# Attention value products taken by pairs of key tiles, denominator sums with them, closing sum one head step sooner

## Chip, cores and metric

One core of one Trainium2 chip runs the whole program. The metric is the device time of one execution in microseconds (us), the median of several. Engine names are those of the profile: PE is TensorE (its matmuls; PEld its weight loads), DVE is VectorE, ACT is ScalarE, POOL is GpSimd, SP is SyncE, which here only issues DMAs.

## What is computed

A decoder layer with three residual blocks, each followed by a layer norm. The change touches only the first, a self attention of 16 heads over 2 batches of 2048 rows with 512 features:

```python
dots = jnp.einsum('bhid,bhjd->bhij', q, k) * scale
dots = jnp.where(causal_mask, -jnp.inf, dots)
attn = jax.nn.softmax(dots, axis=-1)
out = jnp.einsum('bhij,bhjd->bhid', attn, v)
```

Behind it come a cross attention on 77 context rows and a mixture of eight expert networks. The profile has the projections first (to 312 us), then the attention (312 to 1347 us), then the second half.

## The kernel before

`self_attention` goes through 8 groups: 2 batches times 4 groups of 4 heads (a head has 32 features). A group has 4 chunks `c` of 512 query rows, and chunk `c` has 4(c+1) key tiles `kt` of 128 keys; its last four lie on the diagonal, where only 512, 384, 256 and 128 of the queries are needed. That makes 40 tiles (`KU`) and, with a head each, 160 head steps (`VU`) in a group. I write (3,5) for chunk 3, key tile 5. Two groups make a lap, a loop body of 320 steps; a lap starts at step `TAIL` (52).

All engines walk through the same numbered steps `s`, each with its own instructions in a fixed order, and wait for one another by semaphores. A lag says how many steps behind its first matmul a piece of work is issued. `tile_at(s, lag, ...)` gives the tile k whose fourth head step was `lag` steps ago, so it answers at s = 4k+3+lag, and `chunk_at` does so for the last tile of a chunk.

- PE, `scores` (L865, on the diagonal also L868): at step p the transposed scores of one tile and head go to one of three banks of `st_ps` (`RING`), once ACT has read the item three before.
- PE, `aux` (L851): the same products the other way round, for the row maxima of chunks to come, about one in a step, into three banks of `s_ps`. DVE reads each (L804 a full 512 columns, L808 with the mask); PE waits for the item three before. The first `aux` item of a step goes out before the value products, the others behind them. At the end of a chunk's maxima there is a "rows" item (L843), which ACT and DVE turn into two rows of `q_pair`.
- ACT (L762): the exponential of each score bank into `probs`, which holds five tiles (`NP`).
- PE, `values` (L885), lag `VALUES` = 4: the four heads of a tile side by side, 32 columns of the array each, in float32 (two matmul instructions a head), added up in `o_ps`.
- The softmax denominators. Most tiles are in `POOLED`: POOL adds their `probs` (L637) into `total`, one tile at a time, lag 1. Seven tiles of a group are not ((1,2), (2,2), (2,5), (3,2), (3,5), (3,8), (3,11)); for them PE makes `sums` (L899) with a block of ones, lag `SUMS` = 6, again four heads side by side. `totals` (L909), lag `TOTALS` = 12, closes a chunk with one such product over `total`, and waits for POOL's last add of that chunk.
- Behind it, each at its lag counted from `TOTALS`: ACT copies the sums out (`TAKEN[1]`), three small DMAs and a DVE reciprocal spread their inverse, POOL scales the output (`SCALED`, L647), ACT rounds it to half precision (`UPPER`, L777, eight steps later), POOL subtracts (`LOWER`, L652, three more steps), SP stores it. In POOL's step the add comes first, then `SCALED`, then `LOWER`; in ACT's step the exponential comes first, `UPPER` last.

With `TOTALS` = 12, `SCALED` comes at 4k+41, `UPPER` at 4k+49 and `LOWER` at 4k+52 for a chunk that ends with tile k.

Of the kernel before, what the change touches and what calls it, by code (L numbers as in the profile page):

```python
# [401 lines left out]
def self_attention(nc, S, x_rows, q_parts, k_parts, v_rows, o_parts, inv_rows):  # L402
# [29 lines left out]
    NP = 5  # L432
    RING = 3

    VALUES, SUMS = 4, 6
    TOTALS = 12
    TAKEN = VALUES + 1, TOTALS + 1
    DEN_MOVED = TAKEN[1] + 1
    INVERTED = DEN_MOVED + 8
# [78 lines left out]
    def unit_at(s, lag, first, end):  # L518

        p = s - lag  # L520
        return None if (first is not None and p < first) or (end is not None and p >= end) else p

    def tile_at(s, lag, first, end):

        p = unit_at(s, lag, first, end)
        return p // HG if p is not None and p % HG == HG - 1 else None

    def chunk_at(s, lag, first, end):

        k = tile_at(s, lag, first, end)  # L530
        return k // NKU * CPB + CHUNK_OF[k % NKU] if k is not None and k % NKU in CHUNK_OF else None
# [3 lines left out]
    def aux_at(s, first, end):  # L535

        if first is not None:
            reached = [AHEAD + (done_by(TAIL) - AHEAD) * n // TAIL for n in (s, s + 1)]
        else:
            reached = done_by(s), done_by(s + 1)  # L540
        return [n for n in range(*reached) if end is None or n < 2 * NAUX]

    with ExitStack() as stack:
# [286 lines left out]
        def _(pe):  # L830
# [3 lines left out]
            def aux(i, n):  # L834
                what, c, unit = AUX[n % NAUX]
                k = n // NAUX * CPB + c
                slot, a = n % (2 * NAUX) % RING, k // CPB % 2

                pe.wait_ge(s_read.sem, s_read.at(i, before(n, RING, 2 * NAUX)))
                if what == "rows":  # L840

                    pe.wait_ge(max_ready.sem, max_ready.at(i, k))
                    nc.tensor.transpose(s_ps[0:HG * TT, slot, 0:P], row_max[:].rearrange("p h j -> p (h j)"),  # L843
                                        ident_f[:]).then_inc(s_ready.sem, 1)
                    return
                j, h, s = unit
                if j == h == s == 0:

                    pe.wait_ge(qk_loaded[a][c], 6 * 16 * (i + k // (2 * CPB) + 1))
                width = CH if s < c else (j + 1) * P  # L850
                nc.tensor.matmul(s_ps[:, slot, 0:width], q_pair[a][0:NR, c, h, j * P:(j + 1) * P],  # L851
                                 k_pair[a][0:NR, h, s * CH:s * CH + width], start=True,
                                 stop=True).then_inc(s_ready.sem, 1)

            def scores(i, p):
                c, kt, h = VU[p % NVU]
                a, slot = p // NVU % 2, p % (2 * NVU) % RING
                if kt == h == 0:

                    k = p // NVU * CPB + c  # L860
                    pe.wait_ge(rows_moved[k % 2], stored_at(2 * (CPB * i + k // 2 + 1)))
                off = max(kt - c * TT, 0) * P
                pe.wait_ge(exp_done.sem, exp_done.at(i, before(p, RING, 2 * NVU)))
                diagonal = kt >= c * TT
                last = nc.tensor.matmul(st_ps[:, slot, off:], k_pair[a][:, h, kt * P:(kt + 1) * P],  # L865
                                        q_pair[a][:, c, h, off:], start=True, stop=not diagonal)
                if diagonal:
                    last = nc.tensor.matmul(st_ps[:, slot, off:off + P], ident[:], future[:], start=False, stop=True)  # L868
                last.then_inc(st_ready.sem, 1)
# [3 lines left out]
            def values(i, k):  # L873


                c, kt = KU[k % NKU]
                a, off = k // NKU % 2, max(kt - c * TT, 0) * P
                final = k % NKU == LAST_TILE[c]
                if kt == 0:
                    if c == 0:  # L880
                        pe.wait_ge(v_loaded[a], 16 * (i + k // (2 * NKU) + 1))
                    pe.wait_ge(o_taken.sem, o_taken.at(i, k // NKU * CPB + c - 1))
                pe.wait_ge(exp_done.sem, exp_done.at(i, HG * k + HG - 1))
                for h, out in enumerate(heads):
                    last = nc.tensor.matmul(o_ps[out, off:], v_sb[a][:, kt, out], probs[:, k % NP, h, off:],  # L885
                                            start=(kt == 0), stop=final)
                if k % NKU in POOLED[c]:
                    last.then_inc(pv_done.sem, 1)

            def sums(i, k):  # L890

                c, kt = KU[k % NKU]
                if k % NKU in POOLED[c]:
                    return
                opens = all(n in POOLED[c] for n, (x, _) in enumerate(KU) if x == c and n < k % NKU)
                if opens:
                    pe.wait_ge(den_taken.sem, den_taken.at(i, k // NKU * CPB + c - 1))
                for h, out in enumerate(heads):
                    last = nc.tensor.matmul(den_ps[out, :], ones[:], probs[:, k % NP, h], start=opens, stop=False)  # L899
                last.then_inc(pv_done.sem, 1)  # L900

            def totals(i, c):

                opens = all(n in POOLED[c % CPB] for n, (x, _) in enumerate(KU) if x == c % CPB)
                if opens:
                    pe.wait_ge(den_taken.sem, den_taken.at(i, c - 1))
                pe.wait_ge(added.sem, added.at(i, adds_upto(c // CPB * NKU + LAST_TILE[c % CPB]) - 1))
                for h, out in enumerate(heads):
                    last = nc.tensor.matmul(den_ps[out, :], ones[:], total[:, c % 2, h], start=opens, stop=True)  # L909
                last.then_inc(den_ready.sem, 1)  # L910

            def step(i, s, first, end):
                p = unit_at(s, 0, first, end)
                if p is not None:
                    scores(i, p)
                todo = aux_at(s, first, end)
                for n in todo[:1]:
                    aux(i, n)
                k = tile_at(s, VALUES, first, end)
                if k is not None:  # L920
                    values(i, k)
                k = tile_at(s, SUMS, first, end)
                if k is not None:
                    sums(i, k)
                c = chunk_at(s, TOTALS, first, end)
                if c is not None:
                    totals(i, c)
                for n in todo[1:]:
                    aux(i, n)

            pe.wait_ge(const_ready, 2)
            for n in range(AHEAD):
                aux(0, n)
            pe.wait_ge(factors_ready, 2)
            laps(pe, step)


# [581 lines left out]
def layer(nc, x_rows, xT, ctxT, mask, wqkvT, woutT, bout, wq, bq, wk, bk, wv, bv, wo, bo, w1, b1, w2, b2, centroids,  # L1519
          routeT, out):  # L1520

    dram = lambda name, shape, dt: nc.dram_tensor(name, shape, dt).ap()
    q_parts, k_parts, o_parts = (dram(n, [2, D, N], F16) for n in ("q_parts", "k_parts", "o_parts"))
    v_rows = dram("v_rows", [N, D], F32)
    inv_rows = dram("inv_rows", [2, HG, CH], F32)
    w_parts = dram("w_parts", [2 * KT, P, 2, KT * D], F16)
    k_blocks, v_ctx = dram("k_blocks", [B, P, NG * HG * S2], F32), dram("v_ctx", [B, S2, D], F32)
    with ExitStack() as stack:
        S = lasting(nc, stack)
        smalls = [(S["bout_bc"][:], bout.partition_broadcast(P)), (S["bo_bc"][:], bo.partition_broadcast(P)),  # L1530
                  (S["bq_sb"][:], bq), (S["b1_sb"][:], b1), (S["b2_sb"][:], b2)]
        project(nc, S, xT, wqkvT, ctxT, wk, wv, woutT, wq, wo, w1, w2, centroids, routeT, smalls, bk, bv,
                q_parts, k_parts, v_rows, w_parts, k_blocks, v_ctx)
        self_attention(nc, S, x_rows, q_parts, k_parts, v_rows, o_parts, inv_rows)
        second_half(nc, S, x_rows, o_parts, mask, w_parts, k_blocks, v_ctx, out)
# [68 lines left out]
```

## Time and profile before

| | before |
|---|---|
| time, median of 3 (lowest, highest) | 2633.9 us (2633.06, 2635.76) |
| the profiled execution: its time, its span | 2630.97 us, 2629.2 us |
| PE busy over the span | 2430.0 us (92%) |
| DVE busy | 1715.9 us (65%) |
| ACT busy | 1097.3 us (42%) |
| POOL busy | 1119.8 us (43%) |
| matmuls | 13556 |
| granted TensorE clock, mean | 0.958 |

Busy shares are averages over three different stages; the attention is read by itself below. A matmul's duration holds its way through the array (a 512 column one shows 0.38 us, while the next one starts 0.22 us after it), so a PE that is "busy" all the time can still be waiting a little before each matmul. In a timeline the number in square brackets is the idle time of that engine before the instruction, with what ended it; "x2" after an instruction means two of them merged into a line, whose time then spans both.

### The profile page before, as it was taken

What the parts mean: (1) busy time and instruction counts of PE and PEld (TensorE: products, weight loads), DVE (VectorE), ACT (ScalarE), POOL (GpSimd) and SP (SyncE); (2) the same over time, 40 slices, a digit from 0 to 9 for tenths busy, and PEclk for the clock granted to TensorE, in tenths of its full rate; (3) what the DMA queues carried; (4) which work ended last, traced back from release to release, by engine and by line L of the source; (5) the groups of instructions that cost most, each with busy time, mean ns of one, the idle gap of its engine ahead of it and who ended that gap; (6) DMA issues with size and microseconds to landing.
All of it is one profiled execution on the core that took longest, in us unless ns stands there. A gap on an engine that the chain in (4) does not pass through costs nothing. (4 is left out here: it accounts for less than half of the span.)

```text
span 2629.2 us, 42902 instructions
## 1 busy us (share of the span) xinstructions
PE 2430.0 (92%) x13556; PEld 1018.3 (39%) x13556; DVE 1715.9 (65%) x3957; ACT 1097.3 (42%) x2066; POOL 1119.8 (43%) x404
## 2 busy tenths in 40 slices
PE   8999799999999999999956799999999999999998
PEld 3444223332333233323213354444445454454543
DVE  4443687776777677767405477767677776767665
ACT  4331256665666566666623242332324232322420
POOL 0000379988898989898952111102111111101100
PEclk9999799999999999999977899999999999999999
DMA  7864312212121212140021101010100101010000
GB/s 250 294 212 156 89 38 54 58 42 59 42 58 42 63 38 76 28 111 20 25 93 60 45 1 62 1 46 18 41 22 1 63 1 46 17 45 17 1 17 17
DMA packets 130506, 155.66 MB, mean 59 GB/s; under 512 B 19838, under 2 KB 98174, under 8 KB 129245
## 3 DMA queue, kind: packets, MB, share of 16 engines
q1 hardware_dynamic: 130269, 152.69, 18.9%
q8 instruction: 126, 2.06, 0.3%
q14 instruction: 111, 0.91, 0.1%
HBM read 99.96 MB, written 52.17 MB: 58 GB/s over the span
## 5 line engine op out<-in xcount | busy, mean ns | idle before, releaser
L762 ACT ACTIVATE probs<-st_ps 128x512 f32<-128x512 f32 (+3 forms) x1280 | 605.3, 536 | 359.0 <-PE st_ps L865 206.6
L637 POOL TENSOR_TENSOR total<-total,probs 128x2048 f32<-128x2048 f32 (+3 forms) x200 | 706.3, 3531 | 77.8 <-ACT probs L762 65.6
L804 DVE TENSOR_REDUCE seg_max<-s_ps 128x1 f32<-128x512 f32 x768 | 506.2, 684 | 143.4 <-PE s_ps L851 139.9
L865 PE MATMUL st_ps<-q_pair,k_pair 98*128 98x512 f16 (+3 forms) x1280 | 445.5, 362 | 36.6 <-ACT probs L762 22.7
L851 PE MATMUL s_ps<-k_pair,q_pair 96*128 96x512 f16 (+3 forms) x1280 | 446.0, 363 | 31.9 <-DMA q_pair<-q_parts 11.2
L1429 PE MATMUL fps<-x2T,w_p_hi 128*128 128x512 f16 x1024 | 317.3, 379 | 0.0
L885 PE MATMUL o_ps<-probs,v_sb 128*32 128x512 f32 (+3 forms) x2560 | 309.0, 556 | 0.0
L808 DVE CUSTOM_DVE_ANT_0 s_ps<-s_ps,later 128x384 f32<-128x384 f32 (+3 forms) x512 | 250.4, 497 | 89.1 <-issue 85.9
L1429 PE MATMUL fps<-w_p_hi,hT 128*128 128x512 f16 x1024 | 306.1, 381 | 0.0
L865 PEld LDWEIGHTS st_ps<-q_pair,k_pair 98*128 98x128 f16 x1280 | 124.8, 99 | 357.7 <-ACT probs L762 264.7
L1133 POOL TENSOR_TENSOR rstd<-rstd,keep_power 128x4 f32<-128x4 f32 x24 | 26.1, 1090 | 552.0 <-DVE rstd L1254 552.0
L1148 POOL TENSOR_TENSOR soft<-soft,ssum 128x1232 f32<-128x1232 f32 x32 | 72.9, 2287 | 384.4 <-DVE ssum L1284 384.4
L851 PEld LDWEIGHTS s_ps<-k_pair,q_pair 96*128 96x128 f16 x1280 | 126.9, 100 | 227.3 <-DVE seg_max L804 111.4
L1216 ACT ACTIVATE hidden<-fps,keep_b_sb 128x512 f32<-128x512 f32 x128 | 86.4, 686 | 303.7 <-PE fps L1429 303.4
L1391 DVE SCALAR_TENSOR_TENSOR x<-fps,gates_un,x 128x512 f32<-128x512 f32 x256 | 183.9, 745 | 36.2 <-PE fps L1429 33.8
L1429 PE MATMUL fps<-w_p_lo,hT 128*128 128x512 f16 x512 | 194.6, 380 | 0.0
L1429 PE MATMUL fps<-x2T,w_p_lo 128*128 128x512 f16 x512 | 194.0, 379 | 0.0
L637 POOL TENSOR_TENSOR total<-probs 128x2048 f32<-128x2048 f32 (+1 forms) x32 | 136.4, 4263 | 52.8 <-ACT probs L762 52.8
L1380 DVE TENSOR_SCALAR hT<-hidden 128x512 f16<-128x512 f32 x128 | 86.0, 672 | 107.6 <-ACT hidden L1216 107.0
L1429 PEld LDWEIGHTS fps<-x2T,w_p_hi 128*128 128x128 f16 x1024 | 100.2, 98 | 128.8 <-DVE x L1391 5.9
L1429 PEld LDWEIGHTS fps<-w_p_hi,hT 128*128 128x128 f16 x1024 | 98.1, 98 | 131.0 <-issue 20.8
L1187 ACT ACTIVATE soft<-soft 128x1232 f32<-128x1232 f32 x32 | 39.4, 1231 | 200.4 <-DVE soft L1277 200.4
(164 smaller groups left out, 3403.8 us busy)
## 6 DMA issues: line engine op xcount, KB each, us to landing
k_pair<-k_parts SPq DMA_DIRECT2D x96, 128.0 KB, 3.6
q_pair<-q_parts SPq DMA_DIRECT2D x96, 128.0 KB, 4.7
x_raw<-xT_in SPq DMA_DIRECT2D x8, 1024.0 KB, 6.3
q_parts<-qk_out SPq DMA_DIRECT2D x32, 256.0 KB, 3.6
k_parts<-qk_out SPq DMA_DIRECT2D x32, 256.0 KB, 3.9
piece_raw<-w_in SPq DMA_DIRECT2D x8, 1024.0 KB, 8.7
v_rows<-v_out SPq DMA_DIRECT2D x32, 256.0 KB, 2.2
w_parts<-piece_cut SPq DMA_DIRECT2D x8, 1024.0 KB, 5.6
```

Of the source, the lines that this page charges most:

```text
L637: last = nc.gpsimd.tensor_tensor(summed[:, :, off:], other[:, :, off:], probs[:, k % NP, :, off:], ALU.add)
L762: nc.scalar.activation(probs[:, k % NP, h, off:], st_ps[:, p % (2 * NVU) % RING, off:], ACT.Exp, scale=SCALE).then_inc(exp_done.sem, 1)
L804: nc.vector.reduce_max(highest, s_ps[:, slot], AX.X).then_inc(s_read.sem, 1)
L808: nc.vector.tensor_tensor_reduce(s_ps[:, slot, 0:width], s_ps[:, slot, 0:width], later[:, CH - width:CH], 1.0, MASKED, ALU.add, ALU.max, h ...
L851: nc.tensor.matmul(s_ps[:, slot, 0:width], q_pair[a][0:NR, c, h, j * P:(j + 1) * P], k_pair[a][0:NR, h, s * CH:s * CH + width], start=True ...
L865: last = nc.tensor.matmul(st_ps[:, slot, off:], k_pair[a][:, h, kt * P:(kt + 1) * P], q_pair[a][:, c, h, off:], start=True, stop=not diagonal)
L885: last = nc.tensor.matmul(o_ps[out, off:], v_sb[a][:, kt, out], probs[:, k % NP, h, off:], start=(kt == 0), stop=final)
L1148: nc.gpsimd.tensor_tensor(soft[:, j], soft[:, j], ssum[:, j, :].rearrange("p (h a) -> p h a", a=1).broadcast_to([P, H, S2]), ALU.mult).the ...
L1216: nc.scalar.activation(hidden[:, n % 2], fps[:, (u * NUNIT + f) % FB], ACT.Gelu, bias=W["b1_sb"][:, n:n + 1], scale=UN).then_inc(gelu_done ...
L1380: nc.vector.tensor_scalar(hT[:, 0, e % 2, j], hidden[:, n % 2], XS, None, ALU.mult).then_inc(h_hi.sem, 1)
L1391: nc.vector.scalar_tensor_tensor(x2[q][:, j], bank, gates_un[q][:, j, e:e + 1], x2[q][:, j], ALU.mult, ALU.add).then_inc(added.sem, 1)
L1429: last = nc.tensor.matmul(bank, lhs(a, t), rhs(b, t), start=(n == 0), stop=(n == len(steps) - 1))
```

## The change

```diff
-    VALUES, SUMS = 4, 6
-    TOTALS = 12
+    VALUES = 4
+    TOTALS = 11
     TAKEN = VALUES + 1, TOTALS + 1
     DEN_MOVED = TAKEN[1] + 1
...
                 for n in todo[:1]:
                     aux(i, n)
                 k = tile_at(s, VALUES, first, end)
-                if k is not None:
-                    values(i, k)
-                k = tile_at(s, SUMS, first, end)
-                if k is not None:
-                    sums(i, k)
+                if k is not None and k % 2:
+                    for n in (k - 1, k):
+                        values(i, n)
+                        sums(i, n)
                 c = chunk_at(s, TOTALS, first, end)
                 if c is not None:
                     totals(i, c)
```

The value products of an even tile wait for those of the odd tile behind it and go out in the same step, 4k+7 with k odd; a plain sum of either tile stands right behind its value products. The closing sum moves from step 4k+15, where it stood directly behind the value products of tile k+2, to step 4k+14, by itself. Every lag that is counted from `TOTALS` shrinks by one step: `SCALED` 4k+40, `UPPER` 4k+48, `LOWER` 4k+51, and `TAIL`, where a lap starts, 51. No arithmetic is added or taken away.

## Rows read from the trace of the kernel before

**Rows 1.** The attention stretch: busy time (count) by engine, granted clock, DMA share, GB/s

```profile
core 0: us, PE busy (x) PEld busy (x) DVE busy (x) ACT busy (x) POOL busy (x), PEclk, DMA share, GB/s
311.70:1346.70 1035.00, 970.33 (x6309) 312.23 (x6301) 724.08 (x2301) 642.11 (x1397) 918.17 (x302) 0.96 0.19 48
```

**Rows 2.** Timeline around one value product, PE and DVE: start us, us, instruction

```profile
410.78 0.28 PE L851 MATMUL s_ps<-k_pair,q_pair 96*128 96x256 f16 x1
411.00 1.07 PE L885 MATMUL o_ps<-probs,v_sb 128*32 128x512 f32 x8
411.99 0.39 PE L865 MATMUL st_ps<-q_pair,k_pair 98*128 98x512 f16 x1
412.64 0.69 DVE L804 TENSOR_REDUCE seg_max<-s_ps 128x1 f32<-128x512 f32 x1 [0.68 <-PE s_ps L851]
```

**Rows 3.** Timeline of PE: value product and closing sum in one step

```profile
534.36 1.06 PE L885 MATMUL o_ps<-probs,v_sb 128*32 128x512 f32 x8
535.25 1.04 PE L909 MATMUL den_ps<-total,ones 128*32 128x512 f32 x8
536.22 0.39 PE L865 MATMUL st_ps<-q_pair,k_pair 98*128 98x512 f16 x1
```

**Rows 4.** Views by tile: counts, durations min/median/max ns, forms

```profile
L885 PE MATMUL o_ps<-probs,v_sb x2560: 272/592/1063, 311.4 to 1334.0; 128*32 128x512 f32 x137, 128*32 128x384 f32 x20, 128*32 128x128 f32 x20, 128*32 128x256 f32 x20
L899 PE MATMUL den_ps<-probs,ones x448: 592/605/617, 340.1 to 1328.1; 128*32 128x512 f32 x150
L909 PE MATMUL den_ps<-total,ones x256: 592/592/1061, 333.1 to 1346.7; 128*32 128x512 f32 x128
```

**Rows 5.** Timeline of PE: first score products of (3,5) and of (3,9)

```profile
543.71 0.38 PE L865 MATMUL st_ps<-q_pair,k_pair 98*128 98x512 f16 x1
...
556.49 0.39 PE L865 MATMUL st_ps<-q_pair,k_pair 98*128 98x512 f16 x1
```

**Rows 6.** Timeline of DVE: two full reductions; a masked one of 384 columns

```profile
339.85 1.28 DVE L804 TENSOR_REDUCE seg_max<-s_ps 128x1 f32<-128x512 f32 x2
...
417.31 0.56 DVE L808 CUSTOM_DVE_ANT_0 s_ps<-s_ps,later 128x384 f32<-128x384 f32 x1
417.79 0.14 DVE L808 DVE_READ_ACCUMULATOR2_ANT seg_max<- 128x1 f32 x1
```

**Rows 7.** Timeline of POOL in the third group, from (2,3) to (3,3)

```profile
628.91 4.54 POOL L637 TENSOR_TENSOR total<-total,probs 128x2048 f32<-128x2048 f32 x1 [4.71 <-ACT probs L762]
633.40 1.16 POOL L652 TENSOR_TENSOR o_out<-o_sb,o_out 128x512 f16<-128x512 f32 x1
634.51 18.39 POOL L637 TENSOR_TENSOR total<-total,probs 128x2048 f32<-128x2048 f32 x4
652.86 1.27 POOL L647 TENSOR_TENSOR o_sb<-o_raw,inv 128x512 f32<-128x512 f32 x1
654.08 7.21 POOL L637 TENSOR_TENSOR total<-total,probs 128x1536 f32<-128x1536 f32 x3
...
662.37 4.54 POOL L637 TENSOR_TENSOR total<-probs 128x2048 f32<-128x2048 f32 x1
670.09 4.54 POOL L637 TENSOR_TENSOR total<-total,probs 128x2048 f32<-128x2048 f32 x1 [3.19 <-ACT probs L762]
```

**Rows 8.** Timeline of ACT and of PE in the same group, at (3,0)

```profile
654.16 0.63 ACT L777 ACTIVATE o_out<-o_sb 128x512 f16<-128x512 f32 x1 [2.95 <-POOL o_sb L647]
...
655.01 0.39 PE L865 MATMUL st_ps<-q_pair,k_pair 98*128 98x512 f16 x1 [2.17 <-ACT probs L762]
```

**Rows 9.** A stretch behind (3,0) with its granted clock, columns as in rows 1

```profile
655.78:662.61 6.83, 6.83 (x29) 1.73 (x26) 5.40 (x24) 4.05 (x8) 6.67 (x5) 0.50 0.10 23
```

**Rows 10.** Timelines of the second group: POOL, then PE

```profile
489.93 1.17 POOL L652 TENSOR_TENSOR o_out<-o_sb,o_out 128x512 f16<-128x512 f32 x1
...
491.27 1.04 PE L909 MATMUL den_ps<-total,ones 128*32 128x512 f32 x8
...
523.16 0.61 PE L865 MATMUL st_ps<-q_pair,k_pair 98*128 98x512 f16 x1 [2.96 <-ACT probs L762]
```

## The prediction

> **What bounds the kernel now.** I first read the table of windows, to see which engines fill the attention [rows 1]: in 1035 us PE counts 970 us busy, POOL 918, DVE 724, ACT 642. So two engines may set the pace, and the change touches both: PE's order directly, POOL's through the lags. The second half and the projections aren't touched.
>
> Then the timeline of PE around one value product [rows 2]. A score product of 256 columns starts at 410.78 and needs 0.11 us, yet the value product behind it starts at 411.00, not at 410.89: 0.11 us lost on the way in (0.09 to 0.11 elsewhere). Eight instructions then take until 411.99, 0.99 us. What one such product needs by itself is told by the place where two stand together: value product and closing sum take 534.36 to 536.22, 1.86 us, so the second one adds 0.87 [rows 3]. The way out costs 0.99 - 0.86 = 0.14. A block of 32 column products costs 0.24 us of switching.
>
> Counts by tile [rows 4], eight instructions each: 320 value products, 56 plain sums, 32 closing sums. The last stand behind value products, so there are 376 blocks now. After the change there are 160 pairs, which hold the plain sums, and 32 closing sums by themselves: 192. The 184 switches that go are 44 us of PE time.
>
> Last, POOL's timeline, because a busy PE doesn't tell who leads. In the third group [rows 7] POOL works without a gap from 628.91 to 661 us: one add for (2,3), the lower half of an output (`LOWER`), four adds, then the scaling of chunk 1's output (`SCALED`), which ends at 654.13. ACT sits in `UPPER` until then, 2.95 us, and PE behind it, 2.17 us [rows 8]. The granted clock then is 0.50, the lower level of 1.2 GHz, for 6.83 us [rows 9]. So from (2,3) to (3,0) POOL sets the time, whatever PE does. The other even groups look alike. In the odd ones POOL has no gap from (1,3) on, and PE idles 2.96 us at (3,0) [rows 10]. Behind (3,0) PE leads again, with POOL waiting 3.19 us before (3,3) [rows 7]. In the last group POOL is busy to its end; what PE does there is free.
>
> **Part 1, the switches, where PE leads.** I work one stretch through: tiles (3,5) to (3,8), which take 556.49 - 543.71 = 12.78 us [rows 5]. PE's own work in them: 16 score products of 0.22 us, 17 maximum products (13 of 512 columns at 0.22, 4 of 384 at 0.16), 7.0 us; five blocks (four value products, one plain sum) at 0.86 + 0.24, 5.5 us; together 12.5. So PE is nearly the bound there. After: 7.0 + 5 x 0.86 + 2 x 0.24 = 11.8.
>
> But DVE reads the maxima out of three banks, and PE's absence doubles. A full reduction takes 0.60 us of DVE (two in 1.28, one lasting 0.68), a masked one of 384 columns 0.48 (417.31 to 417.79) [rows 6]. DVE's work is 13 x 0.60 + 4 x 0.48 = 9.7 us. After a block DVE starts 0.65 us later than PE (411.99 to 412.64 [rows 2]). At the start of a block it has at most three items, 1.8 us, less some 0.4 that go by while PE issues the last one and switches: 1.4. Around one block it idles 1.0 + 0.65 - 1.4 = 0.25 at the least, around a pair 1.86 + 0.65 - 1.4 = 1.1, around a pair with a plain sum 2.0. Before, DVE's sum was 9.7 + 5 x 0.25 = 11.0, below PE's; after, it is 9.7 + 1.1 + 2.0 = 12.8, above PE's 11.8. The stretch takes 12.8 again. The 0.7 us that PE saves are a wait for DVE.
>
> On the diagonal blocks are short (0.2 to 0.9 us) and DVE isn't starved, so the 0.24 us of each merge stay: three such pairs a group outside POOL's stretch, -0.7. The closing sum loses: it was one block with its neighbour, now it is a block, one head step and a pair. PE pays one switch more and saves one by the pairing, 0; DVE, where it leads, idles 1.0 + 0.4 + 1.86 + 0.65 - 1.4 - 0.6 = 1.9 instead of 1.1 + 0.25, +0.55. I take +0.3 for each of three, +0.9. Sum for a group: about +0.3, for the seven that count +2 us. Its bounds: without starvation some 12 of 23 merges of a group lie outside POOL's stretches, -3.0 a group, -21 us; with starvation worse by 0.3 us in each of nine pairs, +19 us.
>
> **Part 2, POOL's order.** `SCALED` moves from 4k+41 to 4k+40; the add of tile k+9 stands in that step and ahead of it, so POOL's order stays. `LOWER` moves from 4k+52 to 4k+51, and so to the other side of the add of tile k+12. For chunk 0 that is (2,3). In the even groups POOL is idle 4.71 us before that add [rows 7], and `LOWER`, 1.16 us, now fits in there (ACT's `UPPER` is a step earlier too). So `SCALED` of chunk 1 ends 1.16 us sooner after (2,3). PE's own way from (2,3) to (3,0) gets no shorter (part 1), so its wait falls from 2.2 to about 1 us. This holds in three groups; in the seventh no such wait shows.
>
> **Part 3, the clock.** The lower clock stands behind the wait of 2.17 us at (3,0) [rows 8, 9]. If the wait falls to 1 us, I expect the 6.83 us at half clock to go, worth up to 3.4 us of PE work; no row shows a wait of 1 us with nothing behind it, so the bounds are 0 and that. POOL caps that: before (3,3) it works 7.2 + 1.16 + 4.54 = 12.9 of the 15.96 us after 654.13 [rows 7], and the closing sum of chunk 2 waits for its add at 654.08 + 7.2 + 1.16. From there to the add of (3,3): 1.1 + 0.4 (a step) + 1.95 (pair) + four steps and an exponential, 2.4: 5.9, so 14.2 instead of 16.0. Gain 1.8 and the 1.16: 3.0 us in three groups, 9 us.
>
> **Part 4, odd groups.** The closing sum of chunk 1 starts 1.3 us after POOL is free of the last add (its last one ends at 489.93 [rows 10], the sum starts 491.27). It now comes 2.3 us sooner (two value products of 0.86 no longer ahead of it, one step), and the add is 1.16 us later, as `LOWER` now stands before it. PE waits 1.3 - 2.3 - 1.16 = -2.2 us. Queued behind that wait are the next scores, so ACT and DVE. That lies in POOL's stretch, so it takes from the 2.96 us at (3,0) instead of adding to it. What is late next is POOL's `SCALED`, as before. The gain is between 0 and 3 us, by whether the clock falls here instead; I take 1, three times: 3 us.
>
> The other lags: SP's DMAs come one step sooner, and wait for semaphores that are sooner too; the ring of five `probs` holds (an even tile's products come at 4k+11, its buffer is wanted at 4k+20).
>
> **Sum.** Against the profiled execution, 2630.97 us: +2 - 9 - 3 = -10, 2621 us. The median is 2.9 us above that execution: **2624 us**.
>
> **The rivals.** (A) The forecast, POOL's path and the clock give 10 us, the switches nothing: 0.42, with a range of its own of 2617 to 2631.
>
> (B) PE's time counts: DVE keeps up (its reductions are read in the gaps), so each merge outside POOL's stretches pays. 12 x 0.24 x 7 = 21 us and the 12 of parts 2 to 4: 2600. For it: DVE is busy only 70% [rows 1]. Against it: three banks and 1.9 us. 0.10. The Trainium skill has a rule behind this, "TensorEngine Tiling (Array Packing)", section Key Properties: changing the tiling mode drains the array. The rows agree, with 0.24 us for in and out; by the rule alone the time would be 2634 - 44 = 2590.
>
> (C) The switches give nothing and the clock falls all the same: only 1.16 x 3 remain against the +2. 2632, no change: 0.26. For it: no row shows that a wait of 1 us is short enough to keep the clock.
>
> (D) Slower: the closing sum's wait in odd groups is long enough to bring the clock down there. 2.2 us of wait and 3.4 of lost work exceed the 3.0 that POOL's lead leaves, +2.6 in three groups, 8 us; and PE's absence around the closing sum (wait, block, one step, pair) costs DVE its 0.55 in full, 3 x 7 times, 12 us; less 3.5 and the diagonal's 5. With A's clock gain gone: 2646. It decides if PE waits there for some 2 us, as long as the wait that has the lower clock behind it [rows 8, 9]. 0.22.
>
> **Range and chances.** 0.2% is 5 us, about what a measurement of this kernel tells from no change. A reaches from 2617 to 2631 and lies mostly below 2629; so faster 0.10 + 0.38 = 0.48, same 0.04 + 0.26 = 0.30, slower 0.22. The range leaves out the far half of B and the far part of D: 2606 to 2650.
>
> **What the profile after would show.** Part 1: blocks of 16 or 24 instructions, 1.85 or 2.7 us; more idle time of DVE (L804) with PE as releaser; (3,5) to (3,8) still 12.8 us. Part 2: in even groups L652 before the add of (2,3), and less wait of L777 for L647. Part 3: no stretch at 0.5 behind (3,0) there. Part 4: L909 waiting for L637 some 2 us in odd groups. The prediction is wrong if the four tiles take 12.1 (then B), or if new stretches at 0.5 lie at (2,2) (then D).

## The result and the profile after

| | before | after |
|---|---|---|
| time, median | 2633.5 us | 2644.7 us |
| lowest, highest (6 runs each) | 2632.5, 2635.8 | 2643.4, 2647.7 |
| ratio, 95% interval | | 1.0043 (1.003 to 1.0056) |
| span of the profiled execution | 2629.2 us | 2642.9 us |
| last add of POOL in the attention ends | 1345.8 us | 1356.6 us |

The kernel got slower by 11 us, where I had forecast 10 us faster. The time is inside the range; the sign is wrong. The attention ends 10.8 us later; the rest of the span's 13.7 us lies behind it, where nothing was changed. One word on the names: the prediction counts the eight groups from nought, so the first, third, fifth and seventh are its even groups, and the second, fourth, sixth and eighth its odd ones.

The windows of the attention after, in the columns of [rows 1]:

```profile
core 0: us, PE busy (x) PEld busy (x) DVE busy (x) ACT busy (x) POOL busy (x), PEclk, DMA share, GB/s
311.70:1357.00 1045.30, 965.33 (x6307) 335.77 (x6309) 705.81 (x2301) 635.86 (x1398) 918.16 (x302) 0.98 0.19 48
```

The mean clock rose from 0.96 to 0.98, PE is busy less (965 us instead of 970) and yet the stretch is longer. POOL's 918 us are the same. The page's groups of ACT and DVE (busy us, mean ns, idle before with releasers):

```profile
L762 ACT ACTIVATE probs<-st_ps 128x512 f32<-128x512 f32 (+3 forms) x1280 | 593.0, 541 | 383.6 <-PE st_ps L865 210.8
...
L804 DVE TENSOR_REDUCE seg_max<-s_ps 128x1 f32<-128x512 f32 x768 | 502.2, 684 | 174.5 <-PE s_ps L851 172.5
```

DVE's idle time ahead of its full reductions is 174.5 us, 172.5 of it put down to PE's maximum products; ahead of its exponentials ACT idles 383.6. In the page of before these stood at 143.4 and 359.0. Here is one pair of the fourth group, tiles (3,4) and (3,5) with the plain sum of (3,5), on PE, then DVE, then ACT. The line at 803.98 begins with the first score product of (3,5), and the one at 818.33 is that of (3,9):

```profile
803.98 0.60 PE L865 MATMUL st_ps<-q_pair,k_pair 98*128 98x512 f16 x2
...
806.49 0.34 PE L851 MATMUL s_ps<-k_pair,q_pair 96*128 96x384 f16 x1 [0.88 <-DVE seg_max L804]
806.66 0.38 PE L865 MATMUL st_ps<-q_pair,k_pair 98*128 98x512 f16 x1
...
809.21 0.39 PE L851 MATMUL s_ps<-k_pair,q_pair 96*128 96x512 f16 x1
809.53 1.92 PE L885 MATMUL o_ps<-probs,v_sb 128*32 128x512 f32 x16
811.27 1.04 PE L899 MATMUL den_ps<-probs,ones 128*32 128x512 f32 x8
812.24 0.39 PE L865 MATMUL st_ps<-q_pair,k_pair 98*128 98x512 f16 x1
...
818.33 0.39 PE L865 MATMUL st_ps<-q_pair,k_pair 98*128 98x512 f16 x1
...
810.10 0.69 DVE L804 TENSOR_REDUCE seg_max<-s_ps 128x1 f32<-128x512 f32 x1
812.89 0.69 DVE L808 CUSTOM_DVE_ANT_0 s_ps<-s_ps,later 128x512 f32<-128x512 f32 x1 [2.11 <-issue]
...
807.21 1.08 ACT L762 ACTIVATE probs<-st_ps 128x512 f32<-128x512 f32 x2 [0.60 <-PE st_ps L865]
808.76 1.09 ACT L762 ACTIVATE probs<-st_ps 128x512 f32<-128x512 f32 x2 [0.47 <-PE st_ps L865]
812.80 4.03 ACT L762 ACTIVATE probs<-st_ps 128x512 f32<-128x512 f32 x8 [2.95 <-PE st_ps L865]
```

The block is as worked out: 16 + 8 instructions from 809.53 to 812.24, 2.71 us, where 3 x 0.86 + 0.14 is 2.72. DVE has work until 810.78 and is back at 812.89, 2.11 us idle; I had put 2.0. ACT has work for only 0.3 us more when the block starts, idles 2.95 us, and then has eight exponentials in a row in front of it, 4.03 us, for which PE has to wait in its turn. Ahead of the block PE itself waited 0.88 us for DVE, and the score product behind that wait went out only then (806.66). The four tiles (3,5) to (3,8) take 818.33 - 803.98 = 14.35 us in this group, and 13.4 to 14.4 in the first seven, against 12.78 [rows 5].

POOL in the third group, and ACT's `UPPER` there, which answer to [rows 7] and [rows 8]:

```profile
626.25 4.55 POOL L637 TENSOR_TENSOR total<-probs 128x2048 f32<-128x2048 f32 x1 [1.82 <-ACT probs L762]
632.49 1.16 POOL L652 TENSOR_TENSOR o_out<-o_sb,o_out 128x512 f16<-128x512 f32 x1 [1.69 <-ACT o_out L777]
634.03 13.78 POOL L637 TENSOR_TENSOR total<-total,probs 128x2048 f32<-128x2048 f32 x3 [0.39 <-ACT probs L762]
648.22 9.16 POOL L637 TENSOR_TENSOR total<-total,probs 128x2048 f32<-128x2048 f32 x2 [0.41 <-ACT probs L762]
657.34 1.26 POOL L647 TENSOR_TENSOR o_sb<-o_raw,inv 128x512 f32<-128x512 f32 x1
658.56 5.89 POOL L637 TENSOR_TENSOR total<-total,probs 128x1536 f32<-128x1536 f32 x2
...
673.32 9.15 POOL L637 TENSOR_TENSOR total<-total,probs 128x2048 f32<-128x2048 f32 x2 [2.02 <-ACT probs L762]
...
658.63 0.63 ACT L777 ACTIVATE o_out<-o_sb 128x512 f16<-128x512 f32 x1 [1.27 <-POOL o_sb L647]
```

The lower half (L652) now stands ahead of the add at 634.03, in time that was idle. `UPPER` waits 1.27 us instead of 2.95. But POOL itself waits for ACT at 632.49 (1.69 us), and before (2,1) it waits 1.82 us where it had not. The view of waits gives POOL's sums from 312 us on:

```profile
POOL total L637 <- ACT probs L762: 127.8, 71, 16.9
POOL o_out L652 <- ACT o_out L777: 6.0, 4, 2.0
```

For the whole attention I added up POOL's idle time before each instruction from the trace: 115.9 us before, 126.1 after. With a first add 0.7 us later that is the 10.8 us. POOL's own work being the same, the attention's time is POOL's work plus what it waits.

The same by stretches of PE, from the first score product of one tile to that of another, fourth group, in us:

| stretch | before | after |
|---|---|---|
| (0,0) to (1,0) | 9.8 | 10.1 |
| (1,0) to (1,3) | 8.8 | 10.0 |
| (1,3) to (2,0) | 14.1 | 14.1 |
| (2,0) to (2,3) | 9.1 | 10.7 |
| (2,3) to (3,0) | 27.4 | 28.8 |
| (3,0) to (3,3) | 15.3 | 10.7 |
| (3,3) to (3,5) | 7.5 | 7.6 |
| (3,5) to (3,9) | 12.8 | 14.4 |
| (3,9) to (3,13) | 13.6 | 14.5 |
| (3,13) to the next group | 7.7 | 5.7 |
| group | 126.0 | 126.5 |

Most stretches are longer, and two are shorter: the last one by 2.0 us, and (3,0) to (3,3), in which the clock had been at 0.5, by 4.6. In the groups two to seven together these cancel to +2.1 us. The first group is 5.6 us longer and the last, to POOL's last add, 3.0; there more stretches are longer and less comes back.

### The profile page after: what moved, and what is told of

The parts are those of the page before. It is cut to its first block and busy times, and to the rows that moved or that the text cites. A ratio compares the mean times of both kernels' runs of the same rounds, so it can differ in the third digit from the quotient of the medians.

```text
span 2642.9 us, 42908 instructions
## 1 busy us (share of the span) xinstructions
PE 2428.7 (92%) x13556; PEld 1043.6 (39%) x13556; DVE 1698.3 (64%) x3957; ACT 1091.5 (41%) x2066; POOL 1119.9 (42%) x404
## 5 line engine op out<-in xcount | busy, mean ns | idle before, releaser
L762 ACT ACTIVATE probs<-st_ps 128x512 f32<-128x512 f32 (+3 forms) x1280 | 593.0, 541 | 383.6 <-PE st_ps L865 210.8
L804 DVE TENSOR_REDUCE seg_max<-s_ps 128x1 f32<-128x512 f32 x768 | 502.2, 684 | 174.5 <-PE s_ps L851 172.5
L885 PE MATMUL o_ps<-probs,v_sb 128*32 128x512 f32 (+3 forms) x2560 | 278.8, 545 | 0.0
```

What stands on the lines that cost most here:

```text
L762: nc.scalar.activation(probs[:, k % NP, h, off:], st_ps[:, p % (2 * NVU) % RING, off:], ACT.Exp, scale=SCALE).then_inc(exp_done.sem, 1)
L804: nc.vector.reduce_max(highest, s_ps[:, slot], AX.X).then_inc(s_read.sem, 1)
```

## The experiments

Theory S: PE's absence, twice as long, leaves DVE and ACT without work. Theory T: the loss is in the closing sum, the lags and POOL's order.

**One part at a time.** First the pairs without the other lag, and the lag without the pairs:

```diff
 # e1_pairs_only, against the changed kernel
-    TOTALS = 11
+    TOTALS = 12
 # e2_totals_only, against the kernel before
-    TOTALS = 12
+    TOTALS = 11
```

> The changed kernel with TOTALS back at 12: pairs of value products stay, the closing sum goes out in step 4k+15, now behind the pair, and every lag behind it is that of the kernel before. Theory S (the longer absence of PE starves DVE and ACT, whatever the closing sum does): slower than before by as much as the whole change, 2640 to 2650 us, and tiles (3,5) to (3,8) take 13.4 to 14.3 us as in the changed kernel, not 12.8. Theory T (the loss comes from the closing sum by itself and one step sooner, with POOL waited for): about 2634 us, and the four tiles still 13.4, hidden elsewhere.

> The kernel before with TOTALS = 11 alone: value products and plain sums one tile at a time as before, the closing sum a block by itself one step sooner, all later lags one step shorter. Theory S: 2626 to 2636 us, not slower than before, with LOWER of chunk 0 ahead of the add of (2,3) and the idle time of 4.7 us there reduced. Theory T: 2640 to 2648 us.

Measured: pairs alone 2651.3 us, ratio 1.0067 (1.0053 to 1.0081); closing sum alone 2638.0 us, 1.0017 (1.0008 to 1.0026). The pairs are the loss, and worse without the other part, just above the 2640 to 2650 us that S had named; the four tiles (3,5) to (3,8) took 13.3 us and more. So T falls for most of it, though the closing sum by itself costs 4 us, where S had expected nothing. The two don't add: 17 + 4 against 11.

```diff
 # e3_sums_beside, against the kernel before
-    VALUES, SUMS = 4, 6
+    VALUES, SUMS = 4, 4
 # e4_lower_back, against the changed kernel
-    LOWER = UPPER + 3
-    STORED = LOWER + 2
+    LOWER = UPPER + 4
+    STORED = LOWER + 1
```

> The kernel before with SUMS = 4: only the 56 plain sums move, directly behind the value products of their own tile; no pairs, TOTALS 12. It saves 56 switches of 0.24 us (13 us of PE) and makes 56 absences of 1.86 us out of 112 of 1.0 us. Theory S: no gain or slower, 2634 to 2640 us, with the stretch (3,5) to (3,8), which holds one plain sum, at 12.8 to 13.2 us. Theory T: PE's saving shows where POOL leaves room, 2625 to 2632 us.

> The changed kernel with LOWER put back to the other side of POOL's add (LOWER = UPPER + 4, STORED at the same step as in the changed kernel). In the changed kernel POOL waits 5.2 us before the lower halves (before: 0), in return the idle time at (2,3) shrinks. If that order costs more than it brings, this is faster than the changed kernel by 2 to 4 us (2641 to 2643); if it brings what the prediction said, slower by 3 us (2648).

The plain sums beside their own tile give 2631.2 us, ratio 0.9988 (0.9979 to 0.9997): 3 us of the 13 that 56 switches are. PE's extra time ahead of scores rose by 4 us and ahead of maxima by 5, counted as in the table below, so starvation takes most of it already. The time lies 3 us below what S had named and inside T's range, and the four tiles took 12.5 us, where S had 12.8 to 13.2. So S holds for the pairs and is too strong for a value product with its own plain sum behind it. POOL's order put back costs 15 us against the changed kernel: 2660.0 us, or 1.0093 (1.0077 to 1.0108) of the kernel before. I had put its price at 3 to 4 us, and the result lies outside both of the ranges that I had named. POOL's waits for exponentials went from 127.8 us up to 148.0 in that run:

```profile
POOL total L637 <- ACT probs L762: 148.0, 66, 17.0
```

So the place of `LOWER` in POOL's queue is worth far more than the 1.16 us in each of three groups of the forecast. Counted as below, PE has 5 us more ahead of scores in that run than in the changed kernel, 7 more ahead of maxima, and loses 5 more to the lower clock.

**With POOL lightened.** To see what the change does to PE, DVE and ACT, I took half of POOL's adds out of both kernels, then more than half of DVE's reductions too, then half of ACT's exponentials too:

```diff
 # p1, p2: adds over two heads, closing sum over those twice
-nc.gpsimd.tensor_tensor(summed[:, :, off:], other[:, :, off:], probs[:, k % NP, :, off:],
+nc.gpsimd.tensor_tensor(summed[:, 0:2, off:], other[:, 0:2, off:], probs[:, k % NP, 0:2, off:],
 # d1, d2: and half of each reduction (masked ones: only the last 128 columns)
-nc.vector.reduce_max(highest, s_ps[:, slot], AX.X)
+nc.vector.reduce_max(highest, s_ps[:, slot, 0:CH // 2], AX.X)
 # a1, a2: and half of each exponential
-nc.scalar.activation(probs[:, k % NP, h, off:], st_ps[:, p % (2 * NVU) % RING, off:], ACT.Exp,
+nc.scalar.activation(probs[:, k % NP, h, off:half], st_ps[:, p % (2 * NVU) % RING, off:half], ACT.Exp,
```

> The kernel before with POOL's adds over two of the four heads only (the adds of heads 2 and 3 are left out, and the closing sum reads head 0 and 1 twice), which halves POOL's 848 us of adds; nothing else changes. It is the base for the next run. If POOL sets much of the attention's time, it is faster than before by the waits at (3,0), the half clock behind them and the last group's tail: 2570 to 2600 us. If not, 2630 us.

> The changed kernel with the same halved adds of POOL. POOL can no longer set the time, so this against the run before it shows what the change does to PE, DVE and ACT alone. Theory S (DVE starved by the doubled absence of PE eats the switches): slower than that run by 5 to 20 us. Theory T (the loss is POOL's order and its waits): faster than that run by 15 to 40 us, the 44 us of switches.

> The kernel before with POOL's adds halved as above, and DVE's reductions over 256 of 512 columns, masked ones over the last 128 (the rest is left out; PE's products stay whole). PE is then the bound: 5 to 25 us below the run with the adds halved alone. Base for the next run.

> The changed kernel with both reductions of work. Theory S: with DVE's work nearly halved nothing waits for it, and the switches show: faster than the run before it by 15 to 40 us. If ACT is starved as well, by less than 15. Theory T: no further gain over what the pair with POOL halved showed.

> As the run of before with POOL and DVE lightened, and ACT's exponentials over half of each bank's columns too (the other half of probs keeps a constant 1.0 from the start, a fill that lengthens the start alike in both runs of this pair). Base for the next run. PE should be the bound nearly everywhere: 2500 to 2540 us.

> The changed kernel with the same three reductions. In the pair before, PE's waits ahead of score products (for ACT) rose from 21 to 70 us and ate the 44 us of switches, while those ahead of the maximum products (for DVE) stayed at 17. If ACT's starvation is what ate them, this run is faster than its base by 25 to 44 us. If something else lies in the pairs (the array, the clock, the order), by less than 10.

Medians, and where PE's time goes in the trace. The extra time ahead of score (or maximum) products is the sum of their distances from the product before, less what that one needs by its columns (columns / 2400 us + 3 ns at the full clock, twice the columns' part where the granted clock was 0.5), where no block lies between. What those products lost by the lower clock has a column of its own. The blocks' column is the rest: the way into each block, the block, and the time to the next product behind it, with any wait there. Each pair is before's order, then after's, in us:

| | median | difference | ahead of scores (ACT reads them) | ahead of maxima (DVE reads them) | lower clock | blocks |
|---|---|---|---|---|---|---|
| as they are | 2633.5, 2644.7 | +11 | 42, 71 | 51, 93 | 21, 15 | 430, 377 |
| POOL halved | 2571.0, 2610.5 | +39 | 21, 63 | 49, 88 | 4, 12 | 409, 361 |
| and DVE | 2537.5, 2534.6 | -3 | 21, 70 | 13, 13 | 7, 8 | 409, 358 |
| and ACT | 2529.2, 2500.2 | -29 | 15, 35 | 13, 13 | 5, 8 | 408, 357 |

With POOL halved the change costs 39 us, more than S had expected. The sum closes: blocks 48 us less (44 by the price of a switch), 42 more ahead of scores, 39 more ahead of maxima and 8 more by the lower clock make 41, and by the traces the attention is 41 us longer. Lighten DVE, and the waits for it fall to 13 us in both orders, but those ahead of scores still rise by 49 and eat the switches; lighten ACT, and they rise by 20 only, and 29 of the 44 us appear. Why those 20 us are left I have not found out. My expectation for the DVE pair named both outcomes and leaned to the gain; it was the other one. I had also expected the DVE base to be 5 to 25 us below the POOL base, and it was 33.5.

The four tiles (3,5) to (3,8), in before's order and then in after's, in the groups two to six:

| | before's order | after's order |
|---|---|---|
| as they are | 12.8 | 13.4 to 14.4 |
| POOL halved | 12.8 | 13.4 |
| and DVE | 12.5 | 12.0 to 12.3 |
| and ACT | 12.5 | 11.8 |

The last row is what the prediction worked out for PE alone, 12.5 and 11.8. Around its two blocks there DVE idles 2.11 and 0.83 us in the changed kernel, 2.9 together, where the prediction had 3.1; ACT, which it left out, idles 2.95 and 2.08, and with sixteen exponentials of 0.52 us that is 13.3.

Where PE sits idle altogether shows in the view of waits too (engine line, released by: us in total, times, longest). The window is 355 to 1240 us. With POOL halved, before's order and then after's:

```profile
PE s_ps L851 <- DVE seg_max L804: 5.4, 17, 0.4
```

```profile
PE st_ps L865 <- ACT probs L762: 8.6, 30, 0.4
PE s_ps L851 <- DVE seg_max L804: 8.3, 25, 0.4
```

With DVE lightened as well, in the same order:

```profile
PE st_ps L865 <- ACT probs L762: 1.8, 7, 0.3
```

```profile
PE st_ps L865 <- ACT probs L762: 14.0, 48, 0.6
```

These are only the times in which no product is on its way through the array; a product shows 0.38 us where the next can start after 0.22, so of a wait shorter than the 0.16 between them nothing is seen here, which is why I took the distances.

**Where 28 us went.** The change costs 39 us with POOL halved, and 11 as it is. The stretch (3,0) to (3,3) shows where most of that lies: over the first seven groups it takes 99 us before and 67 with POOL halved, but 78 and 76 in the changed order. So POOL at full work cost the kernel before 32 us there, and costs the changed one 1 to 2. ACT's wait at (3,0) was the suspect. I moved `UPPER` four steps on; `LOWER` and the store are counted from it, so they move too:

```diff
 # v1 against the kernel before, v3 against the changed kernel
-    UPPER = SCALED + 8
+    UPPER = SCALED + 12
 # v2: v1, and SUMS = 4
 # v4: v1, and
-    LOWER = UPPER + 3
-    STORED = LOWER + 2
+    LOWER = UPPER + 2
+    STORED = LOWER + 3
```

> The kernel before with UPPER = SCALED + 12 instead of + 8, everything behind it four steps later: ACT's wait for POOL's scaled output comes four head steps later, when POOL should be through. If the 3 us wait of ACT at (3,0) and the half clock behind it cost what the changed kernel's trace shows (the stretch (3,0) to (3,3) fell from 13.8 to 16.6 us to 10.7), this is faster than before: 2612 to 2625 us. If POOL sets the end of that stretch anyway, 2630 to 2634 us.

> The run before this one, and the plain sums directly behind the value products of their tile (SUMS = 4), which alone gave 3 us. If both gains are real and of different places, 3 us faster than with UPPER later alone: 2609 to 2622 us.

> The changed kernel with UPPER = SCALED + 12. If the kernel before hid part of PE's loss behind ACT's wait at (3,0) and its half clock, which both kernels now lack, the change costs more on this base than on its own: 2620 to 2640 us against 2597.7 for the kernel before with the same edit (22 to 40 us). If the hiding has another cause, the difference stays 11 us: 2605 to 2612 us.

> The kernel before with UPPER = SCALED + 12 and LOWER = UPPER + 2, which puts POOL's lower half ahead of the add of its step (STORED stays). If that order is worth something by itself, up to 5 us faster than with UPPER later alone (2592 to 2597 us); if it only helped to unblock ACT, no difference, or some us slower where POOL then waits for ACT (2598 to 2604 us).

Moving it in the kernel before gives 2597.7 us, ratio 0.986 (0.9842 to 0.9878), 37 us faster, against 2612 to 2625 us expected. The windows of its attention, ACT's `UPPER` and POOL in the fourth group:

```profile
311.70:1311.30 999.60, 950.18 (x6306) 308.25 (x6305) 720.75 (x2307) 641.83 (x1399) 917.71 (x302) 0.99 0.19 49
...
766.94 0.63 ACT L777 ACTIVATE o_out<-o_sb 128x512 f16<-128x512 f32 x1 [0.61 <-POOL o_sb L647]
...
765.63 1.27 POOL L647 TENSOR_TENSOR o_sb<-o_raw,inv 128x512 f32<-128x512 f32 x1
766.87 7.24 POOL L637 TENSOR_TENSOR total<-total,probs 128x1536 f32<-128x1536 f32 x3
774.05 1.18 POOL L652 TENSOR_TENSOR o_out<-o_sb,o_out 128x512 f16<-128x512 f32 x1
775.17 4.53 POOL L637 TENSOR_TENSOR total<-probs 128x2048 f32<-128x2048 f32 x1
779.78 4.53 POOL L637 TENSOR_TENSOR total<-total,probs 128x2048 f32<-128x2048 f32 x1
```

The mean clock is 0.99. `UPPER` still waits, but 0.61 us, POOL goes on without a gap from 765.63 into the add of (3,3) at 779.78, where it had waited 3.2 us [rows 7], and (3,0) to (3,3) takes 10 us in the regular groups instead of 14 to 17. Counted as in the table, 17 of the 37 us are the lower clock's loss in the products. That it is `UPPER` and not `LOWER` behind it was not run by itself; v4, with `LOWER` one step sooner again, is no slower.

In the changed kernel the same edit brings 8 us only, 2636.6 us, ratio 1.0013 (1.0004 to 1.0022); its windows:

```profile
311.70:1349.70 1038.00, 968.60 (x6310) 333.64 (x6309) 706.52 (x2309) 639.46 (x1400) 918.24 (x302) 0.97 0.18 47
```

So on this base the change costs 39 us again (2636.6 - 2597.7), as it does with POOL halved. The number is the same, but not all of it is the same loss. By the count of the table v3 has 22 us more than v1 ahead of scores, 42 more ahead of maxima, 6 more by the clock, and only 31 less in blocks, since PE now waits for POOL ahead of the lone closing sums, 9 us of idle time in all. (3,0) to (3,3) takes 13 to 14 us in its groups two to seven, against about 10 in v1. And its clock is 0.97: in six groups a stretch of 3.4 us at half clock begins within 0.6 us of the start of chunk 2's closing sum, ahead of which PE had idled 0.6 to 1.5 us (2.1 in the last group). So v3 shows that the change costs more once the stall at (3,0) is gone, and the POOL pair is the better measure of how much PE, DVE and ACT lose by themselves. Beside it, the plain sums next to their tile (v2) make 2595.0 us, 0.9849 (0.9836 to 0.9863), and POOL's lower half first (v4) 2596.5 us, 0.9855 (0.984 to 0.987); with their intervals neither can be told from v1. v2 and v4 beat both kernels as v1 does, and v1 and v2 lie below the ranges that I had named for them.

## Why the prediction was wrong, point by point

**What bounds the kernel.** Wrong in one half. I had POOL set the time from (2,3) to (3,0), "whatever PE does". With POOL's adds halved that stretch takes 26.9 to 27.4 us, as before in six of the first seven groups, so PE, DVE and ACT need that time anyway. POOL works there without a gap, but what it makes late is `UPPER` at (3,0). Halving the adds gave 63 us all the same: 32 in (3,0) to (3,3), 18 in the last group, most of the rest in the seventh. Nor was the last group free for PE: it is 7 us longer in the changed order with POOL halved. I read ACT's wait at (3,0) as a symptom of POOL's length. But it goes away without any less work on POOL: it is a small instruction, queued ahead of exponentials and waiting for a late engine, and moving it (with `LOWER` behind it) brought 37 us.

**Part 1, the switches, is the step that failed.** The price of a switch was right: the blocks came out to 0.01 us (its 0.14 for the way out is the unrounded value, 0.99 - 0.86 would give 0.13), the four tiles took PE's own 11.8 us when all others were lightened, and then most of the 44 us appear (29). The Trainium skill's rule ("TensorEngine Tiling (Array Packing)", Key Properties: a change of tiling mode drains the array) agrees with these traces, which have 0.24 us for it. It speaks of the array and not of its neighbours. What failed is the starvation term. With it my net for part 1 was +2 us, with an upper bound of +19; it measured 81 us of waits and 8 of lower clock against 48 saved, so with POOL halved the change cost 39. Three things in it were wrong:
- ACT wasn't in the sum. I checked DVE, the fuller of the two, and stopped. Half of the new waits, 42 us, stand ahead of the products that ACT reads, and they are still there with DVE lightened.
- I took the banks to be full when a block begins, 1.4 us of work. At the block shown DVE had 1.2, ACT 0.3: while PE waits for DVE ahead of a maximum product, as at 806.49, the score products behind it don't go out, and ACT's banks run empty first. With DVE lightened ACT had 0.9 us left at that block instead of 0.3, and idled 2.4 us instead of 2.95.
- I compared one sum per engine over four tiles and took the larger, DVE's 12.8. They took 13.4 us at the least with both engines at full work, and 12.0 to 12.3 with DVE lightened. So each engine's sum depends on the other's waits, and the larger one is no bound from above. DVE at full work with ACT lightened was not run, so how much each adds isn't separated.

The bound of 0.3 us a pair had no row behind it, only the hand sum's own error.

**Part 2, POOL's order.** Right in sign, wrong in size: 3.5 us forecast, 15 us by e4. PE's wait at (3,0) in the third group fell from 2.2 to 1.7 us, where I had about 1.

**Part 3, the clock.** Right, and larger than said. Before, seven of the eight groups had 3.4 to 10.2 us of half clock behind (3,0); after, five have none and two of the others 3.4, and the odd groups gained too, where ACT's wait for POOL fell from 3.5 us to 0.9. From (3,0) to (3,3) seven groups became 2 to 6 us shorter. Most of that came with the lags and not with the pairs: over the first seven groups the stretch takes 99 us before, 94 with the pairs alone (e1), 83 with closing sum and lags alone (e2) and 78 with both. (The lags alone pay for it in (2,3) to (3,0), which takes 2 us longer a group in e2.) That is most of what hides the 39 us. I had counted it as gain beside a part 1 of nothing; here it only paid back part of part 1's loss. That the time came to lie inside my range is luck of this kind: part 1's 39 us are far outside the bounds that I had for it. I had expected a wait of 1 us to keep the clock. The length of one wait doesn't decide it: in the third group the changed kernel waits 1.67 us at (3,0) and has no half clock behind it, while v3, in its second group, has 3.4 us of it at a closing sum behind 1.32 us. Its timeline of PE and its windows:

```profile
535.50 1.42 PE L909 MATMUL den_ps<-total,ones 128*32 128x512 f32 x8 [1.32 <-POOL total L637]
...
536.08:539.49 3.41, 3.41 (x22) 0.70 (x18) 0.28 (x1) 1.22 (x3) 3.41 (x2) 0.50 1.15 290
```

**Part 4, the closing sum's wait in odd groups.** 2.2 us forecast in each of three; in those three PE idles 0.6 us each, and all such waits ahead of a lone closing sum are 3.7 us over six of them. PE came later than I had it, which fits part 1's loss. Alone, closing sum and lags cost 4 us (e2).

**The rivals.** D's time, 2646 us, is nearly the measured one, but not its mechanism: it had the clock fall more, and it rose. Of its two parts, the waits at the closing sums are 4 us, where D had 8 with the lost clock in it, and starvation is in every pair, not only around closing sums. B (only PE counts) needs DVE and ACT both lightened. C's 2632 had the starvation at nothing too.

**What stays open.** Why the first group lost 5.6 us, more than the others: its trace has 17 us of half clock against 7, around the heads of its chunks 1 and 2, but I ran nothing that tells whether that is cause or result. How much of the refund at (3,0) is the clock and how much ACT's wait was not separated by a run: v1 removes both. By the table's count the kernel before has 18 us more lower clock than with POOL halved and 21 more ahead of scores, the changed kernel 3 and 7, so the two have about equal parts in the 28 us.

## What to carry to other kernels

A switch saved on a busy engine is paid with the length of its absence: before joining blocks, ask of every engine that it feeds how long its banks last at that moment, and don't take the largest single wait for the whole. Look for short instructions that wait for a late engine at the head of a busy engine's queue; moving one four steps on, with what follows it, gave 1.4%, more than any other edit here that keeps the computation whole. When a change loses less than its parts say, look for a stall that gives something back, and compare stretch by stretch with the stall removed; the totals alone can agree for other reasons.

## What the runs showed of the hardware

Two 32 column float32 blocks of four heads run into each other without a gap, 0.86 us for the second at the full clock, whether the tiles differ (value products of two tiles) or the operands and the bank (value product and plain sum); the first costs 0.24 us more for the way in and out. That I had from one place, and it held in every full-width block at the full clock. Unexpected was the clock: over the attention the granted mean went 0.96, 0.98, 0.99 for before, after and v1, and the kernel with the middle value was the slowest, so a higher clock alone says nothing about who is faster.
